# Layer two's expert tiles in pairs, with their weights fetched from memory by expert number

## The chip, the cores and the metric

The kernel runs on one core of a Trainium2 chip. The metric is the device time of one launch in microseconds, the median of several runs. Below, PE is TensorE, DVE is VectorE, ACT is ScalarE, POOL is GpSimd, and SP is SyncE, which issues most DMAs.

## The reference

Two transformer-like layers on x of 4 x 1024 tokens with 128 channels. Every step adds to the residual stream, and a layer norm stands ahead of it.

```python
# layer one: causal attention with rotary positions, then a top-1 mixture of 8 experts with capacity
out = softmax(mask(rot(x @ wq.T) @ rot(x @ wk.T).T / sqrt(d))) @ (x @ wv.T)
idx = argmax(softmax(xt @ wg)); keep a token if its place in its expert < T / 8
out = gate * (x_token @ W[idx] + b[idx])
# layer two: long convolution by FFT, then a top-2 mixture of 8 experts (H = 256)
y = (x @ Wu + bu) * fftconv(x @ Wv + bv, h) @ Wo + bo
for each of a token's two best experts e, with probability p:
    out += p * (relu(x @ W1[e] + b1[e]) @ W2[e] + b2[e])
```

## The kernel before

All matrices are float32. Tokens lie as 32 tiles of 128. In both mixtures POOL scatters each token's normalized row, with the token's number behind it, to a slot of its expert in device memory (`scatter_rows`, L737: 32 indirect DMAs in layer one, 64 in layer two). SP loads slot tiles of 128 rows, PE works on them, and POOL sends each result tile back to its tokens' places (`send_back`, L746: one indirect DMA per tile). The slot arrays are filled with a far token number before (SP, L660), and the scatter waits for that.

Layer two has 72 expert tiles (`TILES1`). Each belongs to one expert, known only at run time: the routing leaves the number in `expert[0:1, n]` and raises `expert_ready`. A tile goes through these steps, in software pipeline over n:

- SP loads its rows into one of 12 slots (`expert_rows`, L667 for the first 12, then the loop at L673, which waits until the slot's former tile has been sent back).
- ACT copies the expert's weights, 514 columns, from `w12` (all eight experts, held in SBUF) into a ring of three, `w12r` (`copy_weights`, L1006 to L1009). It reads the expert's number into a register first, and waits until the output matmul of the tile three before is done.
- PE transposes the rows (L1323), ACT copies them to `xsT` (L1016), PE makes the hidden layer in PSUM `psS` (two matmuls, each run as two instructions), ACT (even tiles, L1023) or DVE (odd tiles, L1725) adds the bias and takes the relu into `hT`, PE makes the output in `psO`.
- DVE adds the expert's bias b2, again by a register load (L1731), into `ys`, a ring of eight (L1735), and POOL sends `ys` back.

Other work is interleaved in the same loop, at fixed tile numbers. `conv_dve_at`: one of 62 pieces of the inverse transform's additions after each of tiles 0 to 61, on DVE. `conv_pe_at`: four inverse transforms after tiles 0 to 3, and transposes and output projections of the convolution after tiles 32 to 36 and 63 to 67 (L1304, L1718). So DVE's order is: relu of tile n + 1 if odd, addition of tile n, one piece. After the loop SP loads the results of the mixture, DVE, ACT and POOL add them up, SP stores.

`w12` is loaded at L681 once layer two's filter has left that memory (`rad_f`), b2 at L654 as a broadcast to all partitions, ahead of the fills. In SP's queue the order is: inputs, fills, layer two's weights (L681), rows of layer one (L667, L673), matrices of the inverse transform (L696, each behind a forward transform), rows of layer two.

Line 1054 is the helper `mm` for every matmul, so its rows are told apart by their tiles: `psS<-xsT,w12r` is the hidden layer, `psO<-w12r,hT` the output.

## Time and profile before

| | |
|---|---|
| median of 3 runs | 575.92 us (572.16 to 577.34) |
| span of the profiled execution | 571.5 us |
| mean granted clock of PE | 0.851 |
| busy: PE, DVE, ACT, POOL | 381.8, 304.7, 200.2, 285.8 us |
| expert loop of layer two | about 399 to 542 us |
| HBM read, written | 26.18 MB, 24.22 MB |

The span runs from the first to the last instruction; the runs' time also holds what lies around it. Busy times overlap, so no sum of them is a time. What counts is, in each stretch, which wait ends last.

### The profile page before, as it was taken

To read this page: it belongs to the slowest core of one execution; us is meant where nothing else is said; L and a number is where in the kernel's file an instruction comes from. 1 tells how busy PE (TensorE), PEld (TensorE's weight loads), DVE (VectorE), ACT (ScalarE), POOL (GpSimd) and SP (SyncE) were. 2 spreads that over 40 slices of the span, in tenths; PEclk is the share of its full clock that TensorE was granted. 3 is DMA by queue.
4 is the path that set the end of the run, shared out by engine and by line. 5 is a ranking of instruction groups with operands and counts; after the bars stand their busy time and mean duration, and the time that the engine had idled before them with its cause. 6 is when DMAs were issued, how large, how long until landed. Compare 5 with 4: busy or idle time off the path is not lost.

```text
span 571.5 us, 8121 instructions
## 1 busy us (share of the span) xinstructions
PE 381.8 (67%) x2228; PEld 303.4 (53%) x2228; DVE 304.7 (53%) x807; ACT 200.2 (35%) x501; POOL 285.8 (50%) x283
## 2 busy tenths in 40 slices
PE   2583886129698887885994943159977788787700
PEld 0451545028367556685983721137866688677600
DVE  4967593014454486535989920121356576565454
ACT  2461321015133226642220000013665556556351
POOL 2835047732646377501487777720255554565443
PEclk9997998559899699998798975559998889888955
DMA  9999938131221211100001321212122222222084
GB/s 260 383 163 160 189 98 212 55 81 27 75 64 39 65 38 37 38 1 1 5 24 42 108 69 51 69 60 74 35 65 67 72 71 60 72 74 62 10 296 145
DMA packets 63305, 50.27 MB, mean 88 GB/s; under 512 B 7314, under 2 KB 58200, under 8 KB 63006
## 3 DMA queue, kind: packets, MB, share of 16 engines
q1 hardware_dynamic: 56704, 36.92, 27.6%
q0 software_dynamic: 6400, 12.50, 6.7%
q10 hardware_dynamic: 158, 0.33, 0.3%
q8 instruction: 19, 0.31, 0.2%
q14 instruction: 24, 0.20, 0.1%
HBM read 26.18 MB, written 24.22 MB: 88 GB/s over the span
## 4 chain that ended last, share of the span: by engine, by line
PE 31%; DVE 12%; issue 10%; ACT 3%; DMA 2%; ACTq 1%; DVEq 1%; another core or an unknown queue 0%; SPq 0%; POOL 0%; POOLq 0%
PE psS L1054 14%; PE psO L1054 12%; PE psT L1054 2%; PE psT L1323 1%; DMA work<-moe 1%; ACTq L1006 1%; DVE xres L1757 1%; DVE ys L1685 1%; PE psS L1304 1%; ACT row L935 1%; ACT xsT L1016 1%; ACT work L918 0%; DVE work L1690 0%; DVE work L586 0%
## 5 line engine op out<-in xcount | busy, mean ns | idle before, releaser
L737 POOL DMA_INDIRECT slots<-row,slot x96 | 110.0, 1146 | 74.1 <-issue 55.0
L746 POOL DMA_INDIRECT moe<-ys,xs x64 | 63.7, 995 | 103.3 <-DVE ys L1735 58.4
L1054 PE MATMUL psS<-xsT,w12r 128*128 128x128 f32 x288 | 51.9, 307 | 14.6 <-ACT xsT L1016 14.3
L1009 ACT ACTIVATE w12r<-w 128x514 f32 x72 | 45.6, 633 | 34.3 <-PE psO L1054 26.0
L1054 PE MATMUL psO<-w12r,hT 128*128 128x128 f32 x288 | 50.7, 303 | 9.3 <-DVE hT L1725 4.6
L1054 PE MATMUL psS<-work 128*128 128x512 f32 (+3 forms) x96 | 41.5, 545 | 21.1 <-DVE work L1534 11.3
L1054 PEld LDWEIGHTS psS<-xsT,w12r 128*128 128x128 f32 x288 | 42.3, 211 | 20.5 <-ACT xsT L1016 18.7
L1054 PEld LDWEIGHTS psO<-w12r,hT 128*128 128x128 f32 x288 | 42.2, 211 | 12.3 <-issue 11.3
L1559 DVE SCALAR_TENSOR_TENSOR xres<-psO,work,xres 128x128 f32<-128x128 f32 x32 | 11.1, 346 | 66.0 <-remote 43.8
L1054 PE MATMUL psO<-work 128*128 128x128 f32 x288 | 40.3, 286 | 7.2 <-DVE xres L1559 4.5
L1735 DVE TENSOR_TENSOR ys<-psO,b 128x128 f32<-128x128 f32 x72 | 20.8, 289 | 42.2 <-PE psO L1054 31.4
L1158 PE MATMUL psT<-cst,work 128*128 128x128 f32 x144 | 24.9, 299 | 27.2 <-ACT hspec L892 17.2
L1054 PEld LDWEIGHTS psO<-work 128*128 128x128 f32 x288 | 37.2, 201 | 7.7 <-DVE xres L1559 4.7
L928 ACT ACTIVATE work<-psT 128x512 f32<-128x512 f32 (+3 forms) x32 | 16.5, 516 | 69.0 <-PE psT L1158 60.1
L1054 PE MATMUL psS<-xT,mats 128*128 128x256 f32 x96 | 27.2, 410 | 18.1 <-issue 17.7
L1054 PEld LDWEIGHTS psS<-work 128*128 128x128 f32 x96 | 17.9, 213 | 35.9 <-issue 19.1
L1158 PEld LDWEIGHTS psT<-cst,work 128*128 128x128 f32 x144 | 17.0, 152 | 37.1 <-ACT hspec L892 18.1
L994 ACT ACTIVATE work<-psT 128x512 f32<-128x512 f32 x4 | 2.4, 597 | 93.6 <-remote 89.0
L746 POOL DMA_INDIRECT moe<-ys,w x24 | 23.6, 985 | 19.4 <-DVE ys L1735 11.4
L1725 DVE TENSOR_SCALAR hT<-psS,w12r 128x128 f32<-128x128 f32 x72 | 21.7, 343 | 20.0 <-PE psS L1054 19.7
L1054 PEld LDWEIGHTS psS<-xT,mats 128*128 128x128 f32 x96 | 19.0, 204 | 24.2 <-issue 21.8
L1054 PE MATMUL psS<-xT,work 128*128 128x512 f32 x64 | 30.9, 624 | 1.3 <-ACT work L918 0.8
(285 smaller groups left out, 869.3 us busy)
## 6 DMA issues: line engine op xcount, KB each, us to landing
slots<-xs SPq DMA_DIRECT2D x13, 516.0 KB, 14.3
xs<-slots SPq DMA_DIRECT2D x64, 64.5 KB
work<-moe SPq DMA_DIRECT2D x8, 512.0 KB, 4.0
xres<-in_x SPq DMA_DIRECT2D x4, 512.0 KB, 9.3
mats<-in_fw SPq DMA_DIRECT2D x1, 2048.0 KB, 11.3
moe<-xs SPq DMA_DIRECT2D x4, 512.0 KB, 7.4
mats<-in_iv SPq DMA_DIRECT2D x8, 256.0 KB, 2.9
xT<-moe SPq DMA_DIRECT2D x4, 512.0 KB, 8.6
```

What stands on the lines that cost most here:

```text
L737: pool.indirect_dma_start(dst[:, :], bass.IndirectOffsetOnAxis(ap=slots[:, i:i + 1], axis=0), row[:, i, :], None, bounds_check=bound, oob_ ...
L746: pool.indirect_dma_start(dst[:, :], bass.IndirectOffsetOnAxis(ap=row_slots[l][m][:, D:ROWW].bitcast(I32), axis=0), ys[:, n % UNROLL, :], ...
L928: act.activation(pT[n % 2][:, 0:k, :].rearrange("p j q -> p (j q)"), t_bank("p", n, 0)[:, 0:k * P], ACT.Copy).then_inc(pt_act, 1)
L935: act.activation(row[:, i, 0:D], xres[:, i, :], ACT.Identity, bias=nbias[:, i:i + 1], scale=rstd[:, i:i + 1]).then_inc(xn_done, 1)
L1006: e = act.value_load(expert[0:1, n:n + 1], min_val=0, max_val=E - 1)
L1009: act.activation(w12r[:, n % W_RING, :], w12[:, bass.ds(e, 1), :].rearrange("p e h -> p (e h)"), ACT.Copy).then_inc(e_w1, 1)
L1016: act.activation(xsT[:, n % 2, :], TP[n % 2][:, 0:P], ACT.Copy).then_inc(e_xT[1], 1)
L1054: return pe.matmul(o, lhsT, rhs, start=start, stop=stop)
L1158: last = pe.transpose(t_bank("p", n, c)[:, (j - 4 * c) * P:(j - 4 * c + 1) * P], prob[n % 2][:, j * P:(j + 1) * P], ident)
L1559: stt(xres[:, n, :], o_bank("o", n)[:, 0:D], rrec[:, n:n + 1], xres[:, n, :], ALU.mult, ALU.add).then_inc(o_done, 1)
L1725: last = ts(hT[:, n % 2, f, :], S[0][:, n % 2, f * P:(f + 1) * P], w12r[:, n % W_RING, H1 + f:H1 + f + 1], 0.0, ALU.add, ALU.max)
L1735: tt(ys[:, m, :], O[n % 2][:, 0:D], b2[:, bass.ds(e, 1), :].rearrange("p e d -> p (e d)"), ALU.add).then_inc(e_ys[1], 1)
```

## The change

The expert tiles of layer two go in pairs: PE, ACT and DVE take two tiles per step, with a signal per pair (`e_t`, `e_xT`, `e_h`, `e_ha`, `e_hd`, `e_y`, `e_ys`). `xsT`, `hT` and the PSUM tiles hold two tiles per buffer, and DVE's addition covers 256 columns. `w12` is gone. W1, b1, W2 and b2 (already repeated for each partition) are joined into one input of 642 columns per expert, and SP loads each tile's 128 x 642 block from device memory by the expert's number into a ring of eight. ACT's copies and the register loads on ACT and DVE go; SP gets a register load per tile. SP's loops are written out. Its queue now has, after the inverse transform's matrices: eight weight loads, twelve row loads, then for each tile the weights of n + 8 and the rows of n + 12. The loads of the eight experts at L681 and of b2 go, and the wait for the filter moves behind the wait for the scatter.

```diff
-W_RING = 3
-W_COLS = H1 + 2 + 2 * D
+W_RING = 8
+W_COLS = H1 + 2 + 3 * D
...
-            sp.dma_start(b2[:, :, :].rearrange("p e d -> p (e d)"), b2_in.rearrange("e d -> (e d)").partition_broadcast(P)).then_inc(b2_loaded, 16)
...
+            def load_rows(l, src, n):
+                m = n % RING[l]
+                if n >= RING[l]:
+                    wait_sent_back(sp, l, n - RING[l])
+                sp.dma_start(row_slots[l][m], src[n * P:(n + 1) * P, :]).then_inc(xs_loaded[m], 16)
+
+            def load_weights(n):
+                if n >= W_RING:
+                    sp.wait_ge(e_ys[1], (n - W_RING) // 2 + 1)
+                e = sp.value_load(expert[0:1, n:n + 1], min_val=0, max_val=E - 1)
+                sp.dma_start(w12r[:, n % W_RING, :],
+                             w12_in[bass.ds(e, 1), :, :].rearrange("e p h -> p (e h)")).then_inc(w_loaded[n // 2 % (W_RING // 2)], 16)
...
+            sp.wait_ge(expert_ready, 1)
+            for n in range(W_RING):
+                load_weights(n)
             for s in sent1:
                 sp.wait_ge(s, 16 * NT // 2)
-            expert_rows(1, slots1, TILES1)
+            for n in range(RING[1]):
+                load_rows(1, slots1, n)
+            for n in range(TILES1):
+                if n + W_RING < TILES1:
+                    load_weights(n + W_RING)
+                if n + RING[1] < TILES1:
+                    load_rows(1, slots1, n + RING[1])
...
-                pool.wait_ge(e_ys[l], n + 1 if l else n // GROUP + 1)
+                pool.wait_ge(e_ys[l], n // 2 + 1 if l else n // GROUP + 1)
...
-            for n in range(-2, TILES1):
-                if n + 2 < TILES1:
-                    copy_weights(n + 2)
-                if 0 <= n + 2 < TILES1:
-                    take_rows(n + 2)
-                if 0 <= n + 1 < TILES1 and n % 2:
-                    hidden(n + 1)
-                for kind, k in conv_pe_at(n):
+            for p in range(-2, PAIRS1):
+                if p + 2 < PAIRS1:
+                    take_rows(p + 2)
+                if 0 <= p + 1 < PAIRS1 and p % 2:
+                    hidden(p + 1)
+                for kind, k in conv_pe_at(2 * p) + conv_pe_at(2 * p + 1):
...
+            def expert_hidden(p):
+                pe.wait_ge(e_xT[1], p + 1)
+                if p >= 2:
+                    wait_hidden(pe, p - 2)
+                pe.wait_ge(w_loaded[p % (W_RING // 2)], 32 * (2 * p // W_RING + 1))
+                for t in range(2):
+                    n = 2 * p + t
+                    for f in range(2):
+                        last = mm(S[0][:, p % 2, (2 * t + f) * P:(2 * t + f + 1) * P],
+                                  w12r[:, n % W_RING, f * P:(f + 1) * P], xsT[:, p % 2, t * P:(t + 1) * P])
                 last.then_inc(e_h, 1)
...
+            def expert1_out(p):
+                m, w = 2 * p % UNROLL, 2 * p % W_RING
+                for n in (2 * p, 2 * p + 1):
+                    if n >= UNROLL:
+                        wait_sent_back(dve, 1, n - UNROLL)
+                dve.wait_ge(e_y[1], p + 1)
+                tt(ys[:, m:m + 2, :], O[p % 2][:, 0:2 * D].rearrange("p (t d) -> p t d", d=D),
+                   w12r[:, w:w + 2, B2_AT:W_COLS], ALU.add).then_inc(e_ys[1], 1)
```

## Rows read from the trace of the kernel before

**Rows 1.** Stretches: us; PE, PEld, DVE, ACT, POOL busy (instructions); PE clock, DMA share, GB/s.
```profile
92.00:124.00 32.00, 6.49 (x35) 4.62 (x33) 0.00 (x0) 0.60 (x1) 21.38 (x22) 0.58 0.34 93
280.00:328.00 48.00, 38.88 (x214) 32.62 (x212) 44.71 (x86) 5.38 (x9) 40.08 (x27) 0.96 0.18 53
331.00:380.00 49.00, 12.84 (x25) 6.25 (x24) 4.10 (x8) 0.60 (x1) 34.48 (x37) 0.55 0.19 59
...
415.80:463.20 47.40, 34.92 (x236) 31.00 (x235) 29.29 (x79) 27.99 (x80) 25.75 (x27) 0.92 0.26 69
463.20:477.70 14.50, 14.50 (x121) 14.31 (x121) 9.22 (x23) 8.95 (x22) 6.72 (x7) 0.91 0.24 66
```

**Rows 2.** VectorE in order of time: the additions of tiles 5, 31, 37, 63, 71.
```profile
415.84 0.29 DVE L1735 TENSOR_TENSOR ys<-psO,b 128x128 f32<-128x128 f32 x1 [0.85 <-PE psO L1054]
...
463.20 0.29 DVE L1735 TENSOR_TENSOR ys<-psO,b 128x128 f32<-128x128 f32 x1
...
477.72 0.29 DVE L1735 TENSOR_TENSOR ys<-psO,b 128x128 f32<-128x128 f32 x1 [0.49 <-PE psO L1054]
...
523.48 0.29 DVE L1735 TENSOR_TENSOR ys<-psO,b 128x128 f32<-128x128 f32 x1 [0.85 <-PE psO L1054]
...
539.63 0.29 DVE L1735 TENSOR_TENSOR ys<-psO,b 128x128 f32<-128x128 f32 x1 [0.54 <-PE psO L1054]
```

**Rows 3.** Waits, 399 to 542 us: total, times, longest.
```profile
ACT w12r L1009 <- PE psO L1054: 26.0, 21, 2.6
```

**Rows 4.** All engines in order of time: start, us, instruction, idle before.
```profile
448.19 0.61 PE L1054 MATMUL psO<-w12r,hT 128*128 128x128 f32 x4
...
449.44 0.97 POOL L746 DMA_INDIRECT moe<-ys,w  x1 [0.30 <-issue]
...
451.31 0.63 ACT L1009 ACTIVATE w12r<-w 128x514 f32 x1 [2.53 <-PE psO L1054]
451.39 0.29 DVE L1735 TENSOR_TENSOR ys<-psO,b 128x128 f32<-128x128 f32 x1 [2.24 <-PE psO L1054]
...
452.46 0.97 POOL L746 DMA_INDIRECT moe<-ys,xs  x1 [2.05 <-DVE ys L1735]
```

**Rows 5.** GpSimd in order of time: two sends after a gap, the last send.
```profile
426.59 0.97 POOL L746 DMA_INDIRECT moe<-ys,w  x1 [2.03 <-DVE ys L1735]
...
432.14 0.97 POOL L746 DMA_INDIRECT moe<-ys,xs  x1 [2.03 <-DVE ys L1735]
...
541.56 0.97 POOL L746 DMA_INDIRECT moe<-ys,w  x1 [0.31 <-issue]
```

**Rows 6.** Groups of instructions, 399 to 542 us: busy us, mean ns, idle before.
```profile
L1009 ACT ACTIVATE w12r<-w 128x514 f32 x72 | 45.6, 633 | 34.3 <-PE psO L1054 26.0 <-issue 4.4 <-remote 2.8
...
L1462 DVE TENSOR_TENSOR work<-work 128x256 f32<-128x256 f32 x1 | 0.4, 443 | 0.0
```

**Rows 7.** ScalarE's register loads of the expert's number: ns min/median/max.
```profile
L1006 ACTq TENSOR_LOAD <-expert x72: 271/278/481, 398.9 to 535.4; - x72
```

**Rows 8.** DMA issues on the page: KB each, median us to landing.
```profile
mats<-in_iv SPq DMA_DIRECT2D x8, 256.0 KB, 2.9
...
moe<-ys,w12r POOLq DMA_INDIRECT x16, 2.2
```

**Rows 9.** SyncE's queue in order of time: first issue, us for all.
```profile
86.54 6.84 SPq L681 DMA_DIRECT2D w<-in_w  x8
...
385.55 3.66 SPq L667 DMA_DIRECT2D xs<-slots  x8
```

**Rows 10.** PE in order of time: the loop's first two transposes.
```profile
399.58 0.41 PE L1323 MATMUL psT<-cst,xs 128*128 128x128 f32 x2 [0.73 <-issue]
```

**Rows 11.** GpSimd in order of time: the first scatter of layer one.
```profile
77.19 1.75 POOL L737 DMA_INDIRECT slots<-row,slot  x1 [25.32 <-issue]
```

**Rows 12.** The page's slices of 14.3 us: DMA share in tenths, GB/s.
```profile
DMA  9999938131221211100001321212122222222084
GB/s 260 383 163 160 189 98 212 55 81 27 75 64 39 65 38 37 38 1 1 5 24 42 108 69 51 69 60 74 35 65 67 72 71 60 72 74 62 10 296 145
```

More of the change, by code:

```diff
@@ L257, in two_layer_kernel @@
         pickb = sb("pickb", [P, P], BF16)
-        w12 = sb("w12", [P, E, W_COLS])
+        ring = sb("ring", [P, W_RING * W_COLS])
+        w12r = ring[:, :].rearrange("p (n h) -> p n h", h=W_COLS)
         wv = sb("wv", [P, D])
@@ L329, in two_layer_kernel @@
         pT = [part(L, "p (j q) -> p j q", q=P) for _ in range(2)]
-        hx, ht, hg, pe_sb = (w12[:, :, :].rearrange("p e h -> p (e h)")[:, n * L:(n + 1) * L] for n in range(4))
-        fw_small = w12r[:, :, :].rearrange("p n h -> p (n h)")[:, 0:2 * FO + D + 2]
+        hx, ht, hg, pe_sb = (ring[:, n * L:(n + 1) * L] for n in range(4))
+        fw_small = ring[:, 4 * L:4 * L + 2 * FO + D + 2]
         filt_v, filt_spec = ys, hspec
@@ L448, in two_layer_kernel @@
         e_ys = [sem(f"e_ys{l}") for l in range(2)]
-        e_w1 = sem("e_w1")
+        w_loaded = [sem(f"w_loaded{m}") for m in range(W_RING // 2)]
         e_h = sem("e_h")
@@ L1018, in hidden, with take_rows @@
-            def hidden(n):
-                act.wait_ge(e_h, n + 1)
-                if n >= 2:
-                    act.wait_ge(e_y[1], n - 1)
-                for f in range(2):
-                    last = act.activation(hT[:, n % 2, f, :], S[0][:, n % 2, f * P:(f + 1) * P], ACT.Relu,
-                                          bias=w12r[:, n % W_RING, H1 + f:H1 + f + 1])
+            def take_rows(p):
+                act.wait_ge(e_t[1], p + 1)
+                if p >= 2:
+                    act.wait_ge(e_h, p - 1)
+                act.activation(xsT[:, p % 2, :], TP[p % 2][:, 0:2 * P], ACT.Copy).then_inc(e_xT[1], 1)
@@ L1025, in hidden @@
+            def hidden(p):
+                act.wait_ge(e_h, p + 1)
+                if p >= 2:
+                    act.wait_ge(e_y[1], p - 1)
+                for t in range(2):
+                    m = (2 * p + t) % W_RING
+                    for f in range(2):
+                        last = act.activation(hT[:, p % 2, 2 * t + f, :], S[0][:, p % 2, (2 * t + f) * P:(2 * t + f + 1) * P],
+                                              ACT.Relu, bias=w12r[:, m, B1_AT + f:B1_AT + f + 1])
                 last.then_inc(e_ha, 1)
-            act.wait_ge(expert_ready, 1)
@@ new lines, in expert_out @@
+            def expert_out(p):
+                if p >= 2:
+                    pe.wait_ge(e_ys[1], p - 1)
+                wait_hidden(pe, p)
+                for t in range(2):
+                    we = w12r[:, (2 * p + t) % W_RING, W2_AT:B2_AT]
+                    o = O[p % 2][:, t * D:(t + 1) * D]
+                    mm(o, hT[:, p % 2, 2 * t, :], we[:, 0:D], stop=False)
+                    last = mm(o, hT[:, p % 2, 2 * t + 1, :], we[:, D:2 * D], start=False)
+                last.then_inc(e_y[1], 1)
@@ L1351, in _ @@
+            for p in range(-2, PAIRS1):
+                if p + 2 < PAIRS1:
+                    expert_rows(p + 2)
+                if 0 <= p + 1 < PAIRS1:
+                    expert_hidden(p + 1)
+                if 0 <= p:
+                    expert_out(p)
+                for kind, k in conv_pe_at(2 * p) + conv_pe_at(2 * p + 1):
                     {"inv": inverse, "yt": transpose_y, "wo": project_y}[kind](k)
@@ L1740, in _, with expert1_hidden @@
-            back = convolution_back()
-            for n in range(-1, TILES1):
-                if n + 1 < TILES1 and not n % 2:
-                    expert1_hidden(n + 1)
-                if n >= 0:
-                    expert1_out(n)
-                for _ in range(conv_dve_at(n)):
-                    next(back)
-                for kind, k in conv_pe_at(n):
+            def expert1_hidden(p):
+                dve.wait_ge(e_h, p + 1)
+                if p >= 2:
+                    dve.wait_ge(e_y[1], p - 1)
+                for t in range(2):
+                    m = (2 * p + t) % W_RING
+                    for f in range(2):
+                        last = ts(hT[:, p % 2, 2 * t + f, :], S[0][:, p % 2, (2 * t + f) * P:(2 * t + f + 1) * P],
+                                  w12r[:, m, B1_AT + f:B1_AT + f + 1], 0.0, ALU.add, ALU.max)
+                last.then_inc(e_hd, 1)
@@ new lines, in expert1_out @@
+            def expert1_out(p):
[6 more added lines that the diff above has]
+                   w12r[:, w:w + 2, B2_AT:W_COLS], ALU.add).then_inc(e_ys[1], 1)
+            back = convolution_back()
+            for p in range(-1, PAIRS1):
+                if p + 1 < PAIRS1 and p % 2 == 0:
+                    expert1_hidden(p + 1)
+                if p >= 0:
+                    expert1_out(p)
+                for n in (2 * p, 2 * p + 1):
+                    for _ in range(conv_dve_at(n)):
+                        next(back)
+                for kind, k in conv_pe_at(2 * p) + conv_pe_at(2 * p + 1):
```

120 lines of the change are left out of this document (33 added, 87 removed).

## The prediction, made before the change was run

> **What bounds the kernel now.** I read the page's slices first, which show 399 to 542 us as one stage where no engine is full: the expert loop of layer two. The table of stretches [rows 1] cuts it up. In the tile-only stretch from 415.8 to 463.2 PE is busy 35 of 47 us, VectorE 29, ScalarE 28, GpSimd 26; where layer two's output projections sit in the loop, 463.2 to 477.7, PE is full. The additions that end each tile, L1735 [rows 2], give the pace: tiles 5 to 31 (26 of them) take 47.4 us, 1.82 each, tiles 37 to 63 take 45.8, 1.76 each.
>
> Then who waits for whom [rows 3]: ScalarE's weight copy waits 26.0 us, 21 times, for the output matmul that frees its ring of three. It looks as if copy and ring set the pace. In order of time [rows 4] they do not. The output matmul at 448.19 took 0.61 us, yet both that wait for it, copy and addition, start at 451.31 and 451.39, together, 2.5 us late. What runs meanwhile is GpSimd, sends with 0.30 us between, the last at 449.44. The sends alone [rows 5] repeat this: those at 426.59 and 432.14 follow a gap of 2.03 us with two more sends between them: 5.55 us for three. The same is seen where GpSimd scatters rows [rows 1]: in 331 to 380 us it issues 37 scatters and PE gets 25 matmuls done in 49 us; in 92 to 124 VectorE does nothing at all. From 280 to 328 a scatter ran beside a busy PE, so the effect needs more than the scatter, and what more I don't know. I call it a hold: when GpSimd issues indirect DMAs without a pause, what PE signals reaches the others only after that run of sends ends. Worked out from [rows 4]: last send starts at 449.44, the addition at 451.39, the next send at 452.46: 3.0 us from last start to next start. Within a run a send takes 0.97 + 0.30 = 1.275. A cycle of n tiles costs (n - 1) x 1.275 + 3.0; n = 3 gives 5.55, as seen, 1.85 per tile. The two stretches' mean of 1.79 lies 3% under it, since some cycles pass without a hold.
>
> **The change, part by part.** *ScalarE* loses 72 copies of 0.633 us, 45.6 us [rows 6], and 72 register loads of 0.278 [rows 7]. As it is idle for 40% of the stretch and released by the same late signal, I count this at nothing. Without a hold it is worth rival one.
>
> *VectorE* loses its 72 register loads and makes 36 additions of 256 columns, 0.443 each by L1462 [rows 6], for 72 of 0.29: 16 us for 21. The relus are the same work, four in a row instead of two.
>
> *PE* does the same matmuls, 34.9 us busy for 26 tiles, 1.34 each, with the spells at low clock that follow its waits: under any pace below. In the projection stretches it is full and stays so: unchanged.
>
> *GpSimd* has the same 72 sends, but two come ready at once. The first follows its addition by 1.07 us (451.39 to 452.46), here 1.2 for the wider addition, the second 1.275 later. The second pair of a cycle: after its first addition VectorE has two pieces of the convolution, 0.4 to 0.7 us each, in half of the pairs four relus (1.2), then the addition, 1.3 to 2.9 us after the first. GpSimd finishes two sends in 2.55, so mostly runs of four. A third pair needs PE to pass hidden layer, relus and output again (my estimate 4.7 us from the cycle's start, at 0.6 us and more for each group of four matmuls and 1.2 for the relus), when the hold is on. So n = 4: 3 x 1.275 + 3.0 + 0.14 = 6.97 us, 1.74 per tile, and with the same 3%, 1.69. Two stretches of 26 tiles: 47.4 + 45.8 - 52 x 1.69 = **5.3 us saved**.
>
> *First tiles.* The first two pairs share their iterations with four inverse transforms. PE's sum is the same; tile 5 comes perhaps **0.5 us** earlier for three waits less. *Tail:* the last two additions come together; the second send goes 1.2 + 1.275 = 2.5 us after them, where tile 71's went 1.93 after its addition (539.63 to 541.56) [rows 2, 5]: **0.6 us lost**.
>
> *SyncE* takes over. Per tile: a register load of 0.28 to 0.48 [rows 7], the weight load at 0.46 (a plain one, 3.66 / 8) to 0.86 (L681's, 6.84 / 8) and the row load at 0.46 [rows 9]: 1.2 to 1.8 us. I take 1.4, as these are plain loads like the rows. That fits under 1.69, not by much. What is queued: the weights of tile n + 9 stand behind the row load of n + 12, which waits for send n to land, 2.2 us after it, plus its own 0.97; then 1.4 of SyncE and the weights' landing, by 2.9 us for 256 KB [rows 8] some 3.4 for 321: about 8 us from send to weights. PE wants them for tile n + 9 about 1.5 us before the send of tile n + 7: 7 x 1.69 - 1.5 = 10.3 us. Hidden by 2 us; at a pace of 1.4 it is a tie, so this chain bounds a gain too. Ahead of the loop eight weight loads precede the rows: 8 x 0.94 = 7.5 us, so the first row load moves from 385.55 to about 393 [rows 9] and lands by 396; PE's first transpose is at 399.58 [rows 10]. Hidden by 3 us: nothing.
>
> *DMA.* Each tile adds 128 x 642 x 4 bytes, 329 KB, at 1.69 us 195 GB/s on top of 69. The share is 0.26 now [rows 1]. The second slice moved 383 GB/s at 9 tenths or more, the seventh 212 at 8 [rows 12]: by these 0.26 + 0.5 to 0.26 + 0.75, near full at the worse end. I take 0.8, since pieces of 2.5 KB resemble those of the start.
>
> *Early.* 4.2 MB of loads from 85 us on (L681) become four small ones. They lie beside the scatter's hold, which lasts until the scatter's end: nothing. The moved wait on the filter's steps is met by then, as those loads had waited for it at 85. Layer one's row loads lose a loop and keep their waits. One removed load does count: the broadcast of b2, 512 KB, is ahead of the fills of the slot arrays in SyncE's queue while the DMA engines are full (slices one to five [rows 12]), and the scatter waits for the fills, GpSimd idle for 25.3 us until 77.19 [rows 11]. At 383 GB/s that is 1.4 us, at the third slice's 163 it is 3.2. The scatter, and the dead time that ends with it, end that much sooner if PE does as much beside it as before; otherwise nothing. I take **1.5 us saved**.
>
> **Sum.** -5.3 - 0.5 + 0.6 - 1.5 = -6.7, with one short wait fewer (0.3) at each of two projection stretches -7.3. The execution's 571.5 us become 564.2; the median of the runs lies 4.4 above that span, so **568.6 us**.
>
> A rule speaks against this reading. By the Trainium skill, SBUF — State Buffer, "Who interferes with whom", PE and ScalarE never wait on anyone and DMA doesn't contend with a compute engine. The page speaks of ports, and the late signals of [rows 4] are not explained by it; the measurement decides that something holds them. Were the rule the whole truth here, the first rival would hold, whose time comes from rows alone.
>
> **Rivals.**
> 1. *No hold, or one that pairs escape* (faster). The 3 us gap was the old chain of copy, transposed rows, hidden layer and output after all. Then GpSimd's 1.275, VectorE's 29.3 us of 26 tiles less 0.2 each (0.93) with waits, and SyncE's 1.4 bound the pace: 1.4 per tile, 52 x 0.39 = 20 us in place of 5.3: **554**. For it: VectorE and ScalarE lose real work. Against: copy and addition start together, late, 2.5 us after their matmul.
> 2. *Short cycles* (slower). If the hold sets in at each pair's second send, before the next output is signalled, cycles are of two tiles: (1.275 + 3.0 + 0.14) / 2 = 2.21 per tile, +22 us. Half of the cycles so: 1.97, +9 in place of -5.3: **583**. It decides as soon as the next addition starts over 2.6 us after the last one. For it: 1.2 us of relus stand on the path in half of the pairs.
> 3. *Weights late* (same or slower). If they land in 6 us and not 3.4 because the DMA engines are full, the chain above has 10.6 us where 10.3 are there, and the pace rises to 1.8 or 1.9: **574 to 580**.
> 4. *The early loads matter* (faster). VectorE's dead stretch of 92 to 124 sets in while L681's loads are in flight. If they start it, up to 8 us of work beside the scatter come back: **561**.
>
> **Numbers.** Main case 0.38 (own range 562 to 575: 0.22 faster, 0.15 same, 0.01 slower); rival one 0.16, all faster; two 0.20 (0.03 same, 0.17 slower); three 0.14 (half same, half slower); four 0.12, all faster. That sums to 0.50 faster, 0.25 same, 0.25 slower, the bound being 1% (5.8 us), about what a measurement here can tell. The range 552 to 585 leaves a tenth at either end: more than rival one gives, or more short cycles than half.
>
> **What would show it.** GpSimd's sends in runs of four, then 3.1 us; ScalarE's busy time 45 us down; no wait of PE on weights; DMA share near 0.8; 92 to 124 still dead. Runs of two mean rival two; of six or more, or no gaps, rival one; PE waiting for a weight DMA, rival three. The prediction fails first if the hold depends on something that the change alters, such as SyncE's DMAs.

## The result and the profile after

| | before | after |
|---|---|---|
| median of 4 runs | 574.04 us (570.29 to 577.34) | 593.31 us (586.22 to 593.94) |
| span of the profiled execution | 571.5 us | 591.7 us |
| mean granted clock of PE | 0.851 | 0.835 |
| busy: PE, DVE, ACT, POOL | 381.8, 304.7, 200.2, 285.8 us | 390.0, 299.6, 156.1, 290.3 us |

The ratio is 1.042 (95% interval 1.037 to 1.048): slower by 19 us, where 7 us less was forecast. Some executions of a kernel fall into a second, slower state that comes whatever the kernel, so the times and medians below leave out those that were over 1.5% above the fastest of their kernel in a set. In the chain that ended last, DMA has 10% of the span and SyncE's queue 4% (before: 2% and 0%). By engine and by line:

```profile
PE 22%; issue 12%; DVE 11%; DMA 10%; SPq 4%; ACT 2%; POOL 0%; DVEq 0%; POOLq 0%; ACTq 0%
PE psS L1055 11%; PE psO L1055 8%; DMA ring<-in_w 5%; DMA moe<-ys,xs 3%; PE psT L1055 2%; SPq L674 2%; DMA work<-moe 1%; SPq L675 1%; SPq L669 1%; DVE xres L1767 1%; DMA moe<-ys,w 1%; DVE ys L1746 1%; ACT row L945 1%; DVE hT L1736 1%; PE psT L1159 0%
```

L674 is SyncE's register load of an expert's number, L675 the weight load, L669 the row load, L1055 the matmuls, L1746 the addition, L756 the send. The waits from 397 to 565 us (total, times, longest) say who is late now:

```profile
DVE ys L1746 <- PE psO L1055: 44.6, 20, 5.7
PE psS L1055 <- DMA ring<-in_w: 44.6, 21, 4.2
```

TensorE waits 44.6 us for weights, in 21 of the 36 pairs. The stretches, in the columns of [rows 1]: the dead stretch of layer one, layer two's scatters, and the tile-only parts of the loop.

```profile
92.00:124.00 32.00, 12.36 (x63) 9.92 (x62) 1.74 (x6) 2.91 (x7) 18.46 (x19) 0.61 0.23 63
331.00:380.00 49.00, 16.95 (x30) 7.86 (x30) 4.37 (x9) 1.37 (x3) 32.92 (x36) 0.53 0.18 57
414.70:468.00 53.30, 32.02 (x218) 29.42 (x216) 25.32 (x61) 11.43 (x37) 27.05 (x26) 0.87 0.75 207
485.20:538.50 53.30, 34.13 (x244) 31.51 (x242) 27.35 (x66) 12.90 (x41) 26.54 (x25) 0.90 0.74 207
```

The third holds 24 tiles (additions of tiles 6 and 7 at 414.67 to those of 30 and 31 at 467.96), 2.22 us each; the fourth 26 tiles, 2.05 each. Before, tiles 5 to 31 took 1.82 and tiles 37 to 63 took 1.76 [rows 2]. ScalarE is busy 11 and 13 of 53 us there, so the work taken off it is really gone, and the tiles came no faster. The additions that end with tiles 5, 31, 37, 63 and 71, as in [rows 2]:

```profile
412.81 0.41 DVE L1746 TENSOR_TENSOR ys<-psO,ring 128x256 f32<-128x256 f32 x1
...
467.96 0.42 DVE L1746 TENSOR_TENSOR ys<-psO,ring 128x256 f32<-128x256 f32 x1 [1.82 <-PE psO L1055]
...
485.16 0.41 DVE L1746 TENSOR_TENSOR ys<-psO,ring 128x256 f32<-128x256 f32 x1
...
538.48 0.41 DVE L1746 TENSOR_TENSOR ys<-psO,ring 128x256 f32<-128x256 f32 x1
...
558.17 0.42 DVE L1746 TENSOR_TENSOR ys<-psO,ring 128x256 f32<-128x256 f32 x1 [1.08 <-PE psO L1055]
```

Over the same 26 tiles as before the first half's pace is 55.2 / 26 = 2.12. The loop's last send:

```profile
561.69 0.97 POOL L756 DMA_INDIRECT moe<-ys,w  x1 [0.30 <-issue]
```

It starts 20.1 us later than before's [rows 5], and the span is 20.2 longer: all of the loss is in the loop. Tile 5 is 3.0 us earlier than before. Tiles 5 to 31 take 7.8 us more, tiles 37 to 63 take 7.6 more (15.3 in the two tile-only parts, from unrounded times). The two stretches with projections take 2.7 and 3.5 more, and the last send comes 1.6 later after the last addition.

One cycle in order of time shows the chain. First GpSimd, SyncE, PE and VectorE of the changed kernel, from 414 us; the fence after it continues VectorE and GpSimd.

```profile
414.00 0.97 POOL L756 DMA_INDIRECT moe<-ys,xs  x1 [3.05 <-DVE ys L1746]
...
415.27 0.13 SPq L675 DMA_DIRECT2D ring<-in_w  x1
417.92 0.32 SPq L669 DMA_DIRECT2D xs<-slots  x1
419.05 0.58 SPq L675 DMA_DIRECT2D ring<-in_w  x1
...
422.18 1.17 PE L1055 MATMUL psS<-xsT,ring 128*128 128x128 f32 x8 [3.38 <-DMA ring<-in_w]
423.15 1.92 PE L1055 MATMUL psO<-ring,hT 128*128 128x128 f32 x8
```

```profile
425.20 0.42 DVE L1746 TENSOR_TENSOR ys<-psO,ring 128x256 f32<-128x256 f32 x1 [5.34 <-PE psO L1055]
...
426.40 0.97 POOL L756 DMA_INDIRECT moe<-ys,w  x1 [4.19 <-DVE ys L1746]
```

The send of tile 4 starts at 414.00. SyncE stands at the row load of tile 16, which waits for that send to land, until 417.92. Behind it are the weights of tile 13, out at 419.05 and landed at 421.95 by the trace's landing records. TensorE has waited 3.38 us for them with the hidden layer of tiles 12 and 13, and only behind that comes the output of tiles 10 and 11 in its program. Their addition is at 425.20, and the send of tile 10 at 426.40: 12.4 us for six tiles, 2.07 each.

### The profile page after: what moved, and what is told of

It reads as the page before. It is cut to its first block, busy times and chain, and to the rows that moved or that the text cites. A ratio compares the mean times of both kernels' runs of the same rounds, so it can differ in the third digit from the quotient of the medians.

```text
span 591.7 us, 7469 instructions
## 1 busy us (share of the span) xinstructions
PE 390.0 (66%) x2228; PEld 310.6 (52%) x2228; DVE 299.6 (51%) x771; ACT 156.1 (26%) x393; POOL 290.3 (49%) x283
## 4 chain that ended last, share of the span: by engine, by line
PE 22%; issue 12%; DVE 11%; DMA 10%; SPq 4%; ACT 2%; POOL 0%; DVEq 0%; POOLq 0%; ACTq 0%
PE psS L1055 11%; PE psO L1055 8%; DMA ring<-in_w 5%; DMA moe<-ys,xs 3%; PE psT L1055 2%; SPq L674 2%; DMA work<-moe 1%; SPq L675 1%; SPq L669 1%; DVE xres L1767 1%; DMA moe<-ys,w 1%; DVE ys L1746 1%; ACT row L945 1%; DVE hT L1736 1%; PE psT L1159 0%
## 5 line engine op out<-in xcount | busy, mean ns | idle before, releaser
L756 POOL DMA_INDIRECT moe<-ys,xs x64 | 66.1, 1033 | 113.9 <-DVE ys L1746 74.8
L1055 PE MATMUL psS<-xsT,ring 128*128 128x128 f32 x288 | 44.1, 301 | 44.9 <-DMA ring<-in_w 44.6
L1055 PEld LDWEIGHTS psS<-xsT,ring 128*128 128x128 f32 x288 | 38.4, 207 | 50.4 <-issue 40.1
L1055 PE MATMUL psS<-work 128*128 128x512 f32 (+3 forms) x96 | 42.9, 561 | 19.6 <-DVE work L1543 9.3
L1055 PE MATMUL psO<-work 128*128 128x128 f32 x288 | 41.7, 288 | 8.7 <-issue 5.0
L1055 PE MATMUL psO<-ring,hT 128*128 128x128 f32 x288 | 45.6, 311 | 0.5 <-DVE hT L1736 0.4
L1055 PEld LDWEIGHTS psO<-work 128*128 128x128 f32 x288 | 37.7, 203 | 10.1 <-issue 6.1
L1055 PEld LDWEIGHTS psO<-ring,hT 128*128 128x128 f32 x288 | 42.4, 226 | 0.9 <-issue 0.6
L1568 DVE SCALAR_TENSOR_TENSOR xres<-psO,work,xres 128x128 f32<-128x128 f32 x32 | 11.1, 346 | 59.4 <-remote 35.6
L1746 DVE TENSOR_TENSOR ys<-psO,ring 128x256 f32<-128x256 f32 x36 | 15.1, 420 | 49.2 <-PE psO L1055 44.6
L1736 DVE TENSOR_SCALAR hT<-psS,ring 128x128 f32<-128x128 f32 x72 | 20.3, 344 | 38.9 <-PE psS L1055 33.5
L756 POOL DMA_INDIRECT moe<-ys,w x24 | 25.8, 1076 | 25.7 <-DVE ys L1746 19.8
L1055 PEld LDWEIGHTS psS<-work 128*128 128x128 f32 x96 | 18.4, 219 | 34.3 <-issue 19.8
L1055 PE MATMUL psS<-xT,mats 128*128 128x256 f32 x96 | 27.5, 420 | 12.4 <-issue 12.2
L1055 PE MATMUL psS<-xT,work 128*128 128x512 f32 x64 | 32.3, 650 | 1.3 <-ACT work L928 0.8
L1550 DVE TENSOR_REDUCE work<-psS 128x1 f32<-128x128 f32 (+7 forms) x32 | 24.0, 751 | 12.8 <-PE psS L1055 10.7
L1027 ACT ACTIVATE hT<-psS,ring 128x128 f32<-128x128 f32 x72 | 20.5, 368 | 37.0 <-PE psS L1055 32.8
L1055 PEld LDWEIGHTS psS<-xT,mats 128*128 128x128 f32 x96 | 19.9, 211 | 17.8 <-issue 15.3
```

The costliest lines, as they stand in the source:

```text
L756: pool.indirect_dma_start(dst[:, :], bass.IndirectOffsetOnAxis(ap=row_slots[l][m][:, D:ROWW].bitcast(I32), axis=0), ys[:, n % UNROLL, :], ...
L1027: last = act.activation(hT[:, p % 2, 2 * t + f, :], S[0][:, p % 2, (2 * t + f) * P:(2 * t + f + 1) * P], ACT.Relu, bias=w12r[:, m, B1_AT + ...
L1055: return pe.matmul(o, lhsT, rhs, start=start, stop=stop)
L1550: dve.tensor_reduce(negmax[:, n:n + 1], S[n % 2][:, :, :].rearrange("p a m -> p (a m)")[:, 0:(n % J + 1) * P], X, ALU.max, negate=True).th ...
L1568: stt(xres[:, n, :], o_bank("o", n)[:, 0:D], rrec[:, n:n + 1], xres[:, n, :], ALU.mult, ALU.add).then_inc(o_done, 1)
L1736: last = ts(hT[:, p % 2, 2 * t + f, :], S[0][:, p % 2, (2 * t + f) * P:(2 * t + f + 1) * P], w12r[:, m, B1_AT + f:B1_AT + f + 1], 0.0, ALU ...
```

## The experiments

Paces below are the time from the additions of tiles 36 and 37 to those of 62 and 63, divided by 26; for the kernels with single tiles, from tile 36 to 62 (1.80 in the profile before). A signal of TensorE is called late when the semaphore's record is over 0.5 us behind the modelled end of the instruction that makes it. Counts in the loop are for 400 to 540 us. They are good to a few, since where signals are late some of these records are missing from the trace. The comparison of a kernel is with the kernel before in the same set of runs. These sets matter here: the kernel before took 564 to 574 us (medians) in six of them and 507 in one, on a chip that gave 566 in a later set. It was not profiled in the set of 507, but the four kernels that were have no late signal of TensorE there; the kernels profiled where it takes about 570 have them. What makes a set the one or the other was not found. Slips in the expectations: the loop has 72 tiles, so the loads that are left out or changed are those of tiles 8 to 71 and the sends are 72, and a tile's block has 642 columns, not 898 (with its rows 386 KB, not 454).

**A1. Rows asked for four tiles later (507 set).** Both loads of a step are now for tile n + 8.

```
 for n in range(TILES1):
     load_weights(n + 8)
-    load_rows(1, slots1, n + 12)
+    load_rows(1, slots1, n + 8)
```

> The changed kernel with one change of order in SyncE's queue: behind the weights of tile n+8 it issues the row load of tile n+8, which waits for the send of tile n-4, not that of tile n+12, which waits for the send of tile n. Theory (weights late through SyncE's queue): the weights of a pair now wait only for the additions four pairs back, since the sends that a row load waits for landed long ago; TensorE's 44.6 us of waits for the weights fall below 10, the pace of the pairs falls from 2.05 to 2.2 us a tile to 1.55 to 1.8, the loop ends 13 to 25 us earlier and the kernel takes 568 to 580 us (ratio to before 0.99 to 1.01). Rival A (the loads themselves are slow: 52 times 454 KB of weights and rows saturate something): the pace stays above 2.0 and the time at 588 to 594. Rival B (pairs are slower in themselves, through latency of the longer cycle): the waits move from the weights to other rows, the pace stays above 1.95 and the time is above 585.

587.64 us beside 507.36 (ratio 1.159, 1.148 to 1.170): a miss. The waits for weights are gone, but TensorE now waits for rows, 370 to 560 us:

```profile
PE psT L1326 <- DMA xs<-slots: 36.4, 18, 2.9
PEld psT L1326 <- DMA xs<-slots: 21.1, 12, 2.6
PE psT L1326 <- DMA w<-slots: 18.8, 13, 2.6
```

The pace is 2.52. I had put the rows too late: TensorE transposes pair p+4 right behind the output of pair p+1, and the rows leave only after the addition of pair p and both weight loads. Addition to addition two pairs on, that is a cycle of some 10 us for four tiles. So a load's place in SyncE's queue matters both ways: rows that are asked for too late made the pace slower (2.52) than weights that come too late (2.05 in the changed kernel, profiled in another set).

**A2. No weight loads after the first eight (507 set).**

```
-    if n + W_RING < TILES1:
-        load_weights(n + W_RING)
```

> The changed kernel without the weight loads of tiles 8 to 51: the eight tiles loaded first serve for all, so the output of layer two is wrong and only the loop's pace is read. SyncE issues row loads alone and there is no weight traffic. If only the chain through SyncE made the loss, the pace is that of the run with lagged rows, within 0.1 us a tile. If weight traffic or the value loads cost something besides, this run is faster than that one by over 0.1 us a tile (5 us in all). If TensorE's signals are held until a run of sends is over (the hold theory of the prediction) the pace is 1.65 to 1.75 us a tile; without a hold it is bound by GpSimd's sends at 1.25 to 1.4.

The eight blocks loaded first serve all tiles, so the output of layer two is wrong and only the time counts. 513.07 us, ratio 1.011 (1.001 to 1.021), pace 1.37. With pairs and without the weights' fetch the kernel is within 2% of the one before. So pairing costs little in this set. That the fetch is what loses the rest is likely but not shown by this run, as the changed kernel has no time in it. The pace of 1.37 is that of the first rival (1.4), in a set in which its condition, no hold, is met.

**A3, A4. A pause behind each send, or each scatter, in the kernel before (507 set).**

```
 pool.indirect_dma_start(...)
+n_gap[0] += 1
+pool.memset(gap[:, :], 0.0).then_inc(gap_done, 1)
+pool.wait_ge(gap_done, n_gap[0])
```

> The kernel before, with a memset of 48 columns and a wait for it behind every send of layer two on GpSimd (52 of them): GpSimd never issues two sends without a pause. Hold theory: signals of TensorE that now come late, because they are seen only once GpSimd pauses, come after at most one send; GpSimd's wait of about 3 us in each cycle of three sends shrinks, and the loop of 142 us gets 5 to 25 us shorter (time 550 to 570). Rival (nothing is held, the cycle is plain latency of the chain over the engines): each send costs 0.1 to 0.3 us more on the engine that is busy 1.275 of 1.79 us, the time stays within 2 us of before or rises up to 8 us.

> The kernel before, with the same memset and wait behind each of the indirect DMAs that scatter the rows of both layers (32 and 2 times 32): there TensorE and VectorE all but stand still for 17 us and again for some 40 us in the profile of before. Hold theory: with a pause after each scatter the signals of TensorE get through, matmuls and VectorE's work run beside the scatter, and the kernel takes 5 to 30 us less (545 to 570). Rival (nothing is held; the work there waits for the scatter or for loads anyway): the scatters get 0.1 to 0.3 us longer each, 96 of them, and the time rises 3 to 25 us.

549.50 us (1.083, 1.074 to 1.091) and 566.85 (1.119, 1.110 to 1.129). The pause costs 0.16 us of memset and 0.78 of waiting for it. In this set nothing is late, so it can only cost. The second kernel's loop is that of the kernel before, untouched: its pace here is 1.31 where it was 1.80 and 1.77 in the two profiles of before. That is near GpSimd's 1.275 us a send, and GpSimd sends there in runs of 30 and 32 without a pause: with TensorE's signals in time the old kernel's loop is bound by the sends. The two profiles also tell where the 60 us between the sets lie: tile 0 is added at 370.4 in A3, whose scatters are those of the kernel before, where before has 403.6, and the loop from tile 0 to 71 takes 106.8 us in A4 for 136.1.

**A5, A6. Both kernels again, unchanged.**

> The kernel before, unchanged, once more with its profile, beside the kernels of this group: the same kernel took 574 us in one set of runs and 507 us in another. If the late signals of TensorE beside GpSimd's indirect DMAs are a thing of the chip or of the set of runs and not of the program, this profile at 505 to 511 us shows about 16 us of matmuls between 92 and 124 us of the span where the profile at 571.5 us shows 6.49, and the loop of layer two in 110 to 120 us, not 142. If the time is 574 again, the stretches are as in the first profile.

> The changed kernel, unchanged, in the same set of runs as the kernel before. Where TensorE's signals are not late, the kernel before takes 507 us; the chain through SyncE (send, row load, two value loads and weight loads, landing, hidden layer, output, send: 12.4 us for six tiles in the first profile) does not go by TensorE's late signals, so the loop keeps 1.9 to 2.2 us a tile and this kernel takes 560 to 590 us, 10 to 16% more than before. Rival (the late signals made the chain long): the pace falls to 1.6 to 1.8 and the time to 515 to 545.

> The changed kernel again, unchanged, beside the kernels of this group: the pace of 2.08 to 2.2 us a tile, 586 to 594 us. If the set is one in which the kernel before takes 507 us, the chain through SyncE, which goes by sends and landings, keeps the pace above 1.9: 545 to 575 us.

Before took 574.68 us (8 runs) beside 571.86, after 585.47 and 587.27 in the same set, pace 2.08. In a further set after took 600.45 and 607.57, pace 2.09, with before at 566.27 (a single run). The pace of after repeats to 0.04 us. What happens ahead of the loop doesn't: the first scatter of the kernel before is at 77.19 in one execution and 71.7 in the other, its tile 0 is added at 403.6 and 409.9. No run of after fell into a set of 507, so its time there is open.

**A7. Small weight loads.**

```
+cols = W_COLS if n < W_RING else 32
-sp.dma_start(w12r[:, n % W_RING, :], w12_in[bass.ds(e, 1), :, :] ...)
+sp.dma_start(w12r[:, n % W_RING, 0:cols], w12_in[bass.ds(e, 1), :, 0:cols] ...)
```

> The changed kernel with the weight loads of tiles 8 to 51 cut to 32 of 898 columns: the same waits, value loads and DMA instructions in the same order, one twenty-eighth of the bytes; the rest of the weights is stale, so the output of layer two is wrong. If the loss is made by the chain's fixed costs (waits, value loads, issue, a landing that takes 2 us for any size) the pace stays above 1.8 us a tile and the time within 20 us of the changed kernel's. If it is made by moving the bytes (321 KB a tile, landing in 3.8 us), the pace falls to 1.4 to 1.6 and the time to within 15 us of the run without weight loads.

Only 32 of the 642 columns are fetched, so here too the output is wrong and only the time counts. 565.85 us (one run) beside 571.86. Its additions, VectorE in order of time, the first and the last shown being those of tiles 36 and 62:

```profile
470.02 0.41 DVE L1747 TENSOR_TENSOR ys<-psO,ring 128x256 f32<-128x256 f32 x1
...
493.93 0.42 DVE L1747 TENSOR_TENSOR ys<-psO,ring 128x256 f32<-128x256 f32 x1 [3.07 <-PE psO L1056]
496.24 0.41 DVE L1747 TENSOR_TENSOR ys<-psO,ring 128x256 f32<-128x256 f32 x1
500.98 0.42 DVE L1747 TENSOR_TENSOR ys<-psO,ring 128x256 f32<-128x256 f32 x1 [3.39 <-PE psO L1056]
...
513.86 0.42 DVE L1747 TENSOR_TENSOR ys<-psO,ring 128x256 f32<-128x256 f32 x1
```

They come two and two, 2.3 us and then 4.7 apart: cycles of four tiles. 26 tiles take 43.84 us, 1.69 each, with 21 of 86 signals late in the loop. This is the pace that the prediction had, reached once the weights land mostly 1.4 to 1.9 us after their issue and not 2.5 to 4.2. It lies between the two expectations (over 1.8, and 1.4 to 1.6). A shorter landing takes most of the loss away, though the queue's order is unchanged; TensorE still waits 23.4 us for weights. In the first half (tiles 5 to 31) the pace is 1.74, and the kernel before has 1.72 and 1.73 for the two parts in the profile of the same set, so no gain over it is shown.

**A8. ScalarE issues the weight loads.** After the hidden layer of each pair it waits for the addition, loads the register and issues two loads; SyncE keeps the rows.

> The changed kernel with the weight loads of tiles 8 to 51 (wait for the addition, value load, DMA) issued by ScalarE behind the hidden layer of the pair, and only the row loads left on SyncE. No weight load stands behind a row load that waits for a send. If the loss is the place of the weight loads behind row loads, TensorE's waits for the weights shrink by more than half and the time is 20 to 50 us below the changed kernel's. If it is the ring's depth (the addition of pair p to the weights of pair p+4: value loads, landing, hidden layer, output), the gain is below 15 us, since ScalarE pays the same value loads and landings; and ScalarE, with 2 us more a pair, may then be late with its own copies.

567.84 and 575.95 us beside 571.86 for before, and 585.47 and 587.27 for after. Waits for weights fall from 39.9 to 13.3 us, the pace to 1.85, and from tile 7 to 31 to 1.78 (after: 2.28). The gain of 15 us lies at the border of the two expectations. So a queue of its own is worth most of the loss. That ScalarE pays for it, as the pace of 1.85 suggests, was not taken apart.

**A9, A10. SyncE's order by pairs.**

```
-for n in range(TILES1):
-    load_weights(n + 8);  load_rows(1, slots1, n + 12)
+for n in range(0, TILES1, 2):
+    load_weights(n + 8);  load_weights(n + 9)
+    load_rows(1, slots1, n + 10);  load_rows(1, slots1, n + 11)   # A9
+    load_rows(1, slots1, n + 12);  load_rows(1, slots1, n + 13)   # A10 instead
```

> The changed kernel with SyncE's order in the loop by pairs: both weight loads of pair p+4, then the row loads of pair p+5 (of p+6 in the changed kernel, each behind one weight load). A row load now waits for a send of pair p-1, which has landed before the addition of pair p+1; so no weight load stands behind a send that has not landed, and rows still come one pair before TensorE wants them. Theory (weights late through the queue and their landing): the addition of pair p is at 0, both weight loads are out by 2.7, landed by 6.3, and TensorE wants them after the output of pair p+2 at two pairs' time, 6.8: the wait of 40 us for the weights falls under 10, the pace from 2.08 to 1.65 to 1.8 us a tile, the time to 562 to 576 us where the kernel before takes 572. Rival (321 KB of weights a tile are too much traffic in 1.69 us, whatever the order): landing takes longer as the pace rises, the pace stays at 1.9 or more and the time at 580 or more.

> As the run by pairs, but the row loads stay those of pair p+6, which wait for the sends of pair p: only the second weight load of a pair moves ahead of the first row load. The chain from the send of tile 2p+1 over its landing to the weights of pair p+5 is as in the changed kernel, two tiles shorter in what it issues behind the send. If waiting for fresh sends in front of weight loads is the cause, this run keeps most of the loss: pace 1.9 to 2.1, time 578 to 592 where the kernel before takes 572. If the number of value loads between a send and the landing were the cause, it would gain as much as the run by pairs.

> The order by pairs again, in another set of runs. Where TensorE's signals come late (the kernel before at 566 to 584 us): 562 to 583 us, within 2% of the kernel before. Where they don't (the kernel before at 505 to 511 us): GpSimd's sends would allow 1.29 us a tile, the weights come 2.7 us of issue and 3.6 us of landing behind the addition of pair p, and are wanted one output and two pairs later, so the pace is set by them at 1.5 to 1.7 and the time is 520 to 545 us, slower than the kernel before by 3 to 7%.

A9 took 567.01 and 571.49 us, A10 584.39 and 592.94, where before took 566.27 and after 600.45 and 607.57. In another set A9 took 569.08 (8 runs) beside 567.80, ratio 1.000 (0.995 to 1.006). SyncE in A9:

```profile
430.61 1.46 SPq L675 DMA_DIRECT2D ring<-in_w  x2
432.11 0.94 SPq L669 DMA_DIRECT2D xs<-slots  x2
434.15 1.14 SPq L675 DMA_DIRECT2D ring<-in_w  x2
435.33 1.33 SPq L669 DMA_DIRECT2D xs<-slots  x2
```

Nothing stands between a pair's loads. The view of waits has no row of TensorE for the weights any more, only 24 us for rows; the pace is 1.74 in both runs. A10, whose row loads still wait for the sends just made, keeps 32.9 us of waits for weights and a pace of 1.98. The two orders issue the same loads. What differs is which sends the row loads ahead of the weights wait for: that is the cause. A saturated memory isn't, since A9 moves more in the same time, 224 GB/s for 207, at a DMA share of 0.78:

```profile
400.00:530.00 130.00, 99.91 (x757) 92.95 (x755) 71.45 (x168) 38.26 (x112) 70.15 (x67) 0.93 0.78 224
```

**A11. Pauses behind every scatter and send, in a set near 570.**

> The kernel before with the memset and its wait behind every scatter of both layers and every send of layer two. In a set of runs where the kernel before takes 507 us (no late signals) it loses as the two single edits did, 8% and 12%, in all some 600 us or less. Where the kernel before takes 572 us: by the hold theory TensorE's signals come through in each pause, so more than 12 us of matmuls run between 92 and 115 us and the loop's pace stays at or below 1.8 us a tile: 540 to 572 us. If a pause of 0.8 us doesn't let them through, the edit costs as in the other set: 590 to 640 us.

613.15 us beside 566.27. No signal of 136 is late in the loop, where each send has its pause (50 of 202 in the profile before), and layer one's scatter no longer stops the others:

```profile
92.00:124.00 32.00, 13.59 (x119) 13.03 (x118) 3.28 (x11) 6.56 (x16) 18.85 (x34) 0.77 0.30 81
```

Against [rows 1] there are 119 matmuls for 35, and 16 instructions of ScalarE for one. The loop's paces, 1.57 in its first half and 1.80 in its second, are those of A3 in the 507 set (1.61 and 1.82). So a pause with a wait takes the hold away. The same execution holds the counter-test: the 32 sends of layer one's experts have no pause, and there, from 140 to 195 us, 17 of 45 signals are late, by up to 6.6 us (14 of 40 in the profile before). At 0.94 us behind each of 168 the pauses cost more than the hold: the time is that of the case in which they were expected to let nothing through (590 to 640). The price is paid in the scatters, since tile 0 is added at 437.6 for 403.6, while the loop takes 133.3 us for 136.1.

**A12, A13. A memset with no wait behind every scatter and send,** on A9 and on the kernel before.

> The order by pairs, with a memset of one column behind every scatter and send on GpSimd, and no wait for it, so that two indirect DMAs never follow each other directly but the pause is under 0.2 us where the memset with its wait took 0.9. Hold theory in its narrow form (any other instruction between two indirect DMAs lets TensorE's signals through): in a set with late signals none is late by over 0.5 us any more, matmuls run beside both scatters, and the time is 515 to 550 us. Rival (it was the wait of 0.8 us and not the instruction that let them through): the signals stay late, and 184 memsets add 10 to 25 us: 580 to 600 us.

> The kernel before with the same memsets. Narrow hold theory: in a set with late signals it falls from 572 to 515 to 545 us. Rival: it rises to 580 to 600 us. In a set without late signals it only costs: 515 to 535 us beside 507.

573.65 and 573.39 us beside 567.80. In the loop of A12 11 of 104 signals are late (A9: 16 of 93), and 48 of 199 in that of A13, as before. The narrow form of the hold theory is wrong: 515 to 550 us were expected from it, and a memset between two indirect DMAs leaves the signals late, where a memset with a wait does not.

**A14 to A16. The pause behind every fourth scatter (on A9), every eighth (on A9), every fourth (on the kernel before).**

```
+if i % 4 == 3:
+    n_gap[0] += 1
+    pool.memset(gap[:, :], 0.0).then_inc(gap_done, 1)
+    pool.wait_ge(gap_done, n_gap[0])
```

> The order by pairs, with a memset and a wait for it behind every fourth scatter of both layers (24 of 96), none behind the sends. A wait costs GpSimd about 0.9 us, so 22 us more of scatter if the scatters bound the time. If TensorE's signals get through in each wait, none is later than about five scatters (6 us) and TensorE, VectorE and ScalarE work beside the scatter; the gain is up to the 65 us that separate the two kinds of sets, shared between what the pauses cost and what the overlap gives: 545 to 570 us where the kernel before takes 570. Rival (scatters bound these stretches anyway): 580 to 595 us.

> The same with a wait behind every eighth scatter (12 of 96): 11 us of pauses at most. If what counts is that signals get through now and then, 555 to 570 us; if they must come through within two or three scatters, nothing is gained and 572 to 585 us is what the pauses cost.

> The kernel before with the memset and wait behind every fourth scatter, and nothing of the change. If the gain of the order by pairs with these pauses (556 us beside 566 to 590) comes from the pauses in the scatters alone, this run gains the same 2 to 4% against the kernel before, in a set of runs in which that takes 566 to 590 us. If the pauses need the changed kernel (loads of layer two that are no longer in the scatter's way, or weights already in the ring), it gains under 1% or loses. In a set where the kernel before takes 507 us, 24 pauses of 0.9 us cost 10 to 22 us.

A14 took 551.63 to 558.27 us beside 565.91 to 572.78, ratio 0.978 (0.963 to 0.993); A15, beside the same, 562.76 to 568.61, ratio 0.995 (0.984 to 1.006); A16, in another set, 554.80 to 561.42 beside 562.01 to 568.14, ratio 0.989 (0.979 to 0.999). A14 in the dead stretch:

```profile
92.00:124.00 32.00, 18.19 (x131) 15.58 (x131) 3.80 (x14) 7.09 (x17) 17.93 (x23) 0.83 0.21 58
```

131 matmuls there, and tile 0 is added at 384.7, 12 to 30 us before the profiles of after and A9. Its loop is no faster than A9's (pace 1.76). So A14 is 1 to 4% faster than the kernel before, in a set with late signals. But A16 has the pause without the change and gains too, by 0.1 to 2%. The intervals of the two overlap, so nothing shows that the change has a part in the gain.

## Why the prediction was wrong

**The step that failed** is in SyncE's paragraph: weights of tile n+9 are wanted "about 1.5 us before the send of tile n + 7: 7 x 1.69 - 1.5 = 10.3 us. Hidden by 2 us". In the profile they are wanted 4.2 us before the send of tile n+6 (422.18 to 426.40): TensorE runs the hidden layer of a pair before the output of the pair ahead of it, and both tiles of a pair wait for the later weights. That leaves 6 x 1.69 - 4.2 = 5.9 us, for a chain which I had put at 8 and which measured 7.95 (414.00 to 421.95). It is late by 2.1 us in six tiles, 0.34 a tile, and 1.69 + 0.34 = 2.03 is near the pace of the second half (2.05). That is one cycle of the loop; from one send to that six tiles on, the cycles in the tile-only parts take 11.1 to 15.3 us. The term was 0; it is 0.34 x 52 = 18 us. With the two tile-only parts 5.3 us faster as forecast and 15.3 slower as measured, the miss there is 20.6 us, so 18 of it is this step. Two kernels with the same loads and another order bear the cause out (A9, A10), as does one with the chain shortened (A7).

The span came out 27.5 us above the forecast of 564.2. Beside the 20.6, the two stretches with projections account for 6.8: I had them unchanged, with PE full, less 0.6, and they took 6.2 us more. PE is busy 14.0 of 17.2 us there in the first and 16.3 of 19.7 in the second. In other profiles of after the first takes 13.1 and 13.9 us, so only the second is a steady loss (19.7 and 22.6 for 16.1), and its cause was not taken apart. What is left cancels: tile 5 came 1.0 us earlier than forecast, the last send 1.0 later after its addition.

**The chain's own terms** were right in sum and off in parts. A landing at 3.4 measured mostly 2.5 to 4.2 us. From the start of a send to the row load that waits for it I had 3.2 us; it took 3.9. SyncE's tile at 1.4 us: in A9 two weight loads and the register load between them take 1.46 from the first's start to the second's end and two row loads 0.94, and the tiles of after follow each other in 1.5 to 1.6 where nothing blocks them.

**Cycles of four at 1.69** are not what the changed kernel does. Of its 22 runs of sends with over 1 us of idle between them, 13 are of two sends, 4 of four and 5 of six, and the hold hardly acts: 2 of 89 signals are late in the loop, while GpSimd waits for additions that wait for weights. Such cycles do come in A7, with 21 of 86 signals late: from tile 38 to 57 its sends go by fours, at a pace of 1.69. But the forecast gain of 5.3 us is not shown. A9, which no longer waits for weights either, is level with the kernel before at a pace of 1.74 for 1.80 and 1.77. A7's span of 564.0 beside the sum's 564.2 is partly chance, with before's runs 7 us apart.

**Rival three** was the right mechanism with a wrong size. I gave it 574 to 580 and the condition that loads take 6 us because the DMA engines are full. They take some 3.2 as a rule; the share is 0.75, near the 0.8 that I took. The weights were late because the time that was there had been counted too long, not because the loads are slow. Weighing it by the landing alone, I gave it 0.14. The measured 593 lies outside its range.

**Rival two** (cycles of two) is in the sends, but not by its cause. Its sign came, runs of two and additions over 2.6 us apart, as in the sends of tiles 11 and 12, which follow the one at 426.40:

```profile
427.67 0.97 POOL L756 DMA_INDIRECT moe<-ys,w  x1 [0.30 <-issue]
431.74 0.97 POOL L756 DMA_INDIRECT moe<-ys,xs  x1 [3.10 <-DVE ys L1746]
```

What it says to be behind them, a hold at each pair's second send, would show as late signals, and there are 2 of 89. What ends the wait is the weights. Taken by the sends alone, this profile would have been read as rival two.

**Rival four** (the early loads start the dead stretch) has no support: those loads are gone, VectorE is busy for 1.74 us of 32, and tile 5 comes 3.0 us earlier where 8 were at stake. But the stretch differs between executions of one kernel. The kernel before has 48 matmuls and 7.7 us of VectorE there in its second profile, and after 87 matmuls in its second, so a small part is not ruled out. **Rival one's** 1.4 is measured at 1.37 (A2), but only where no signal is late and without the fetch.

**ScalarE at nothing** was right as far as runs show: 44 us less busy, and A9, which has this and no waits for weights, gains nothing on the kernel before. **VectorE** lost 5.1 us of busy time, as said. **Early**: the first scatter is 3.5 us earlier in the profile, 1.5 were forecast, but the same kernel differs by 5.5 us there between two executions, so this term was neither shown nor refuted. **Tail**: 561.7 us of last send and 591.7 of span leave 30.0, before had 29.9. From the last addition to the last send it takes 3.5 us where 2.5 were forecast, as three sends were still due and not two: 1.6 us lost for 0.6.

The Trainium skill's rule that PE and ScalarE never wait on anyone (SBUF — State Buffer, "Who interferes with whom") stands beside A11 and the 507 set: what is late is a signal, and no run here shows whether an access to memory is. So the rule may hold and still not forecast these 60 us.

**What stays open:** what makes TensorE's signals late in one set and not in another on the same chip; what after takes in a set of 507; why a wait of 0.78 us lets signals through where a memset of 0.13 doesn't; and what slowed the stretch with the last projections.

## What to carry to other kernels

When loads move to one in-order queue, write down for each kind of load the event that it waits for, and put nothing urgent behind a wait for something just issued: here the same loads in another order were worth 29 us or more in the set that had both orders (600.45 and 607.57 to 567.01 and 571.49), and 0.3 us a tile in the pace. Work the slack out from the consumer's program order, not from the ring's size: a ring of eight tiles used in pairs, with the next pair's first layer ahead of this pair's second, gave six tiles minus 4.2 us. An engine with idle time that is released by the same late event has nothing to give, even with 45 us of work taken off it (A9).

## What the runs showed of the hardware that I had not expected

The same kernel takes 507 or 570 us by the set of runs, one chip having shown both. What differs between the profiles of the two kinds of sets is TensorE's semaphores beside GpSimd's indirect DMAs. In the loop 50 of 202 are late by up to 2.2 us in the profile before, 45 of 188 by up to 3.1 in its repeat, and none in the four kernels of the 507 set; beside the sends of layer one 14 of 40, by up to 6.6 us. VectorE's and ScalarE's signals are in time in both. With GpSimd waiting 0.78 us behind each indirect DMA none is late there, while the sends of the same execution without the wait still have late ones; one column's memset changes nothing. The same stretch in the 507 set, here of A2, has 123 matmuls for the 35 of [rows 1]:

```profile
92.00:124.00 32.00, 16.13 (x123) 14.30 (x122) 3.24 (x11) 6.37 (x17) 19.07 (x20) 0.76 0.22 61
```

A memset of 128 x 48 behind an indirect DMA takes 0.16 us, and GpSimd's wait for it 0.78 us more.
